# A two-layer decoder on one core: more of layer 0's output stage moved into its attention, and another order of the memory hops

## The reference

```
x = layernorm(x + quaternion_attention(x))      # 16 heads of 16, softmax over 1024 keys
x = layernorm(x + memory_hops(ctx, x, W0, W1))  # two hops over 77 context rows
x = layernorm(x + experts(x))                   # 8 experts, 256 rows each, gelu
x = layernorm(x + long_convolution(x))          # layer 1 starts here
x = layernorm(x + cross_attention(x, ctx))      # 16 heads
x = layernorm(x + quantised_gated_ffn(x))
```

## Time and profile before

| | |
|---|---|
| median of three runs | 780.7 us |
| the profiled execution | 774.46 us, span 772.7 us |
| PE matmul busy | 698.3 us, 90% |
| ACT busy | 557.5 us, 72% |
| DVE busy | 492.1 us, 64% |
| POOL busy | 193.3 us, 25% |
| mean granted TensorE clock | 0.986 |

### The profile page before, as it was taken

How to read it: one execution, slowest core, us unless ns; L and a number is a source line. 1 busy time by engine, 2 the same in 40 slices (tenths; PEclk the granted TensorE clock), 3 DMA queues, 4 the chain that set the end, 5 groups by cost and what they waited for, 6 DMA issues and landing times.

```text
span 772.7 us, 10924 instructions
## 1 busy us (share of the span) xinstructions
PE 698.3 (90%) x3854; PEld 383.6 (50%) x3854; DVE 492.1 (64%) x1156; ACT 557.5 (72%) x1071; POOL 193.3 (25%) x234
## 2 busy tenths in 40 slices
PE   4999999989999999989999999967988999993897
PEld 2652222212222223879888887633454644441686
DVE  4794645663422133669527666767887787988786
ACT  3759999999999997464242434799987633799991
POOL 1661143210110000203352232455554200000022
PEclk9999999999999999999999999999999999997899
DMA  7412112241157142203156000002000000000002
GB/s 195 140 31 49 30 28 69 28 96 28 28 111 230 29 115 77 102 8 111 46 172 215 5 0 1 1 1 82 7 35 1 1 1 0 1 0 0 1 27 82
DMA packets 58606, 42.27 MB, mean 55 GB/s; under 512 B 38226, under 2 KB 55352, under 8 KB 58424
## 3 DMA queue, kind: packets, MB, share of 16 engines
q1 hardware_dynamic: 58408, 41.44, 19.5%
q10 hardware_dynamic: 144, 0.13, 0.1%
HBM read 28.72 MB, written 4.46 MB: 43 GB/s over the span
## 4 chain that ended last, share of the span: by engine, by line
PE 55%; ACT 24%; DVE 15%; issue 3%; DMA 1%; SPq 1%; POOL 0%; POOLq 0%; ACTq 0%; DVEq 0%
ACT arena L665 12%; PE banks L1673 9%; PE banks L2210 8%; PE banks L1972 7%; PE banks L1988 6%; PE banks L1659 4%; ACT arena L790 4%; PE banks L1643 3%; DVE arena L1498 2%; DVE arena L1063 2%; PE banks L1833 2%; PE banks L1646 2%; DVE arena L1071 2%; PE banks L2002 1%; PE banks L1716 1%
## 5 line engine op out<-in xcount | busy, mean ns | idle before, releaser
L665 ACT ACTIVATE arena<-banks 128x1024 f32<-128x1024 f32 x256 | 239.8, 1047 | 6.7 <-PE banks L1673 4.2
L1673 PE MATMUL banks<-arena 128*32 128x512 f32 x1024 | 136.4, 604 | 2.6 <-DVE arena L1139 2.4
L1659 PE MATMUL banks<-arena 64*128 64x512 f16 x512 | 86.4, 383 | 10.3 <-ACT arena L665 5.8
L2210 PE MATMUL banks<-arena 128*128 128x512 f32 x192 | 83.1, 594 | 1.1 <-DVE arena L1514 0.9
L790 ACT ACTIVATE arena<-banks,arena 128x77 f32<-128x77 f32 x256 | 70.6, 403 | 13.9 <-DVE arena L1413 13.7
L414 POOL TENSOR_SCALAR arena<-arena 128x2 f32<-128x2 f32 (+2 forms) x39 | 11.8, 302 | 254.9 <-DVE arena L1066 254.9
L1659 PEld LDWEIGHTS banks<-arena 64*128 64x128 f16 x512 | 21.0, 93 | 108.8 <-ACT arena L665 98.9
L746 ACT ACTIVATE arena<-banks,arena 128x256 f32<-128x256 f32 x64 | 26.9, 471 | 49.3 <-PE banks L1972 49.3
L2210 PEld LDWEIGHTS banks<-arena 128*128 128x128 f32 x192 | 36.2, 190 | 47.4 <-issue 43.4
L1988 PE MATMUL banks<-arena 128*128 128x256 f32 x256 | 56.5, 380 | 1.2 <-ACT arena L687 1.2
L1972 PE MATMUL banks<-arena 128*128 128x256 f32 x256 | 56.2, 379 | 0.0
(11 more groups left out here) (255 smaller groups left out, 1253.4 us busy)
## 6 DMA issues: line engine op xcount, KB each, us to landing
arena<-in_L_ffn_w SPq DMA_DIRECT2D x16, 1024.0 KB, 7.5
w_kept<-arena SPq DMA_DIRECT2D x3, 768.0 KB, 3.6
arena<-w_kept SPq DMA_DIRECT2D x3, 768.0 KB, 4.4
arena<-in_x SPq DMA_DIRECT2D x4, 512.0 KB, 7.1
out_x<-arena SPq DMA_DIRECT2D x3, 512.0 KB, 2.9
arena<-in_L_ffn_b SPq DMA_DIRECT2D x1, 1024.0 KB, 14.9
arena<-in_L_ffn_w_gate SPq DMA_DIRECT2D x1, 768.0 KB, 7.6
arena<-in_L_ffn_w_up SPq DMA_DIRECT2D x1, 768.0 KB, 9.4
```

Of the source, the lines that this page charges most:

```text
L665: act.activation(PT[kt % 2][:, half], PS[:, 2 * (n % 3):2 * (n % 3) + 2, :], ACT.Exp, scale=DH ** -0.5 / QK_UP ** 2).then_inc(sem("exp_don ...
L1659: mm = pe.matmul(bank(2 * (n % 3) + h), KT[u % 2][64 * h:64 * h + 64, P * kt:P * kt + P], QT[u % 2][64 * h:64 * h + 64, 512 * half:512 * h ...
L1673: mm = pe.matmul(PS[32 * j:32 * j + 32, 6, :], VS[w][:, kt, h, :], PT[kt % 2][:, half, h, :], start=(kt == 0), stop=(kt == TB - 1))
L2210: mm = pe.matmul(bank(2 + n % 4), (wgT if n < IC * G4 else wuT)[:, k, P * c:P * c + P], XT[:, k, 512 * g:512 * g + 512], start=(k == 0), s ...
```

## The change

- Batch 0's output stage takes ten key steps for each q (Q_STEPS): turns at 0 and 2, the turn back at 4, projections at 5 to 8. It ends in unit 12. The turn of the next q waits for the residual's addition (first_y) instead of its statistics. VectorE's pieces, the quantisation of the last weight among them, are placed anew in units 8 to 13.
- Unit 13 turns groups 0 and 1 of the normalised rows (early_x_turn, steps 2, 4, 6, 7), copied by VectorE (early_x) instead of by ACT behind the attention.
- Unit 14 turns the first four of batch 1's head pairs, for all four q (early_turn, part 0), unit 15 the next three (part 1, steps 0, 2, 4, 6), and in it, at steps 3 and 5, two matrices of layer 1 (l1_turn 0 and 1, copied by VectorE in early_weight). They wait for the four matrix loads alone (l1_raw_in). All use bank 7. Behind the attention only the last head pair is turned (last_turn, last_heads).
- Behind the attention, scores of set 0 stand ahead of batch 1's output stage, and those of sets 1 and 2 right behind it. VectorE weaves minimum and weights into that stage. The hops have another order, and mem_residual(1), mem_stats(1) and mem_residual(2) stand ahead of the last mem_summed; before, they stood behind it. The first FFN matmul waits for two residuals instead of one.
- WpT, WqT and bc1 lie elsewhere in SBUF, and mem_output uses other banks.

The diff, cut to its core (indentation shortened; left out are SBUF places, the removed VectorE loop, ACT's list, and the removed functions of PE):

```diff
-MEM_ORDER = ((0, 0), (0, 1), (0, 2), (0, 3), (1, 0), (0, 4), (1, 1), (0, 5), (1, 2), (1, 3), (1, 4), (1, 5))
+MEM_ORDER = ((0, 0), (0, 1), (0, 2), (1, 0), (0, 3), (1, 1), (0, 4), (1, 2), (0, 5), (1, 3), (1, 4), (1, 5))
 MEM_AT = {item: i for i, item in enumerate(MEM_ORDER)}
-L1_BANK = (4, 5, 0, 0, 0)
-MEM_OUT = ((2, 2), (4, 3), (6, 5), (4, 6))
+L1_BANK = (7, 7, 0, 0, 0)
+MEM_OUT = ((2, 2), (2, 3), (4, 5), (6, 6))
 HT = 13
 SPREAD = {2: (0, 0), 4: (1, 0), 6: (0, 1), 8: (1, 1), 11: (0, 2), 13: (1, 2)}
+Q_STEPS = 10
+EARLY_X_AT = (2, 4, 6, 7)
+EARLY_AT = (0, 2, 4, 6)
+EARLY_L1_AT = (3, 5)
 UX = T * KD
...
+def early_x(g, k):
+    if k == 0:
+        dve.wait_ge(sem("x_tr"), T + g + 1)
+    else:
+        dve.wait_ge(sem("xg_tr"), MEM_X + g + 1)
+    dve.tensor_copy(XT[:, k, 512 * g:512 * g + 512], bank(7)).then_inc(sem("xgT" if k else "xT"), 1)
+def early_heads(part, i):
+    dve.wait_ge(sem("o_tr"), 9 + 4 * part + i)
+    n = 4 - part
+    o = bank(7)[:, 0:P * n].rearrange("p (u j w) -> p u j w", u=n, j=4)
+    link(dve.reciprocal(rden0[:, 0:n], o[:, :, :, DH]))
+    for half in range(2):
+        ins = dve.tensor_tensor(ATT1[:, i, half, P * part:P * part + 2 * DH * n].rearrange("p (u h d) -> p u h d", u=n, h=2),
+                                o[:, :, half::2, 0:DH], rden0[:, 0:n, half::2, None].to_broadcast([P, n, 2, DH]), ALU.mult)
+    ins.then_inc(sem("att"), 1)
...
+    dve.wait_ge(sem("o_tr"), 17)
...
+        ins = dve.tensor_tensor(ATT1[:, :, half, 2 * DH * (NP - 1):2 * DH * NP].rearrange("p q (h d) -> p q h d", h=2),
+                                o[:, :, half::2, 0:DH], rden0[:, :, half::2, None].to_broadcast([P, 4, 2, DH]), ALU.mult)
+    ins.then_inc(sem("att"), 1)
...
+def early_weight(n):
+    dve.wait_ge(sem("l1_wtr"), n + 1)
+    dve.tensor_copy((WpT, WqT)[n].rearrange("p k d -> p (k d)"), bank(7)).then_inc(sem("l1_wT"), 1)
...
+    if r < 4:
+        dve.sem_inc(sem("first_y"), 1)
...
         late_qn(HT if u == HT - TB else T - 1)
     if late < T and u % 2 == 1:
         late_v(late)
-    if u >= NP:
-        q = (u - NP) // 2
...
+    if u == NP:
+        first_heads(0, 0)
+        first_heads(0, 1)
+        quantised(2, 1)
+        first_turned(0)
+    if u == NP + 1:
+        out_residual(0, 7)
+        first_heads(1, 0)
+        out_norm(0)
+        quantised(2, 2)
+        first_heads(1, 1)
+        first_turned(1)
+    if u == NP + 2:
+        out_residual(1, 7)
+        first_heads(2, 0)
+        out_norm(1)
+        first_heads(2, 1)
+    if u == NP + 3:
+        first_turned(2)
+        out_residual(2, 7)
+        first_heads(3, 0)
+        out_norm(2)
+    if u == NP + 4:
+        first_heads(3, 1)
+        first_turned(3)
+        out_residual(3, 7)
+    if u == NP + 5:
+        out_norm(3)
+        for g in range(2):
+            for k in range(KD):
+                early_x(g, k)
+    if u == NP + 6:
+        for i in range(4):
+            early_heads(0, i)
+    if u == NP + 7:
+        early_heads(1, 0)
+        early_heads(1, 1)
+        early_weight(0)
+        early_heads(1, 2)
+        early_weight(1)
+        early_heads(1, 3)
     dve.wait_ge(sem("pv_done"), TB * u + TB)
     dve.tensor_copy(OSB[:, u], bank(6)).then_inc(sem("o_evac"), 1)
...
     view = lambda j: X[:, 4 * g + j, :]
     normalise(view, view, 4, 4 * (g % 2)).then_inc(sem("ln_b"), 1)
+last_heads()
 mem_lowest(0, 0)
+out_residual(4, 6)
+mem_weights(0, 0)
+out_residual(5, 7)
+out_norm(4)
+out_residual(6, 6)
+out_norm(5)
+out_residual(7, 7)
 mem_lowest(0, 1)
-mem_weights(0, 0)
+out_norm(6)
 mem_lowest(0, 2)
 mem_weights(0, 1)
+out_norm(7)
+mem_lowest(1, 0)
+mem_weights(0, 2)
 mem_lowest(0, 3)
-mem_weights(0, 2)
-mem_lowest(1, 0)
+mem_weights(1, 0)
+mem_lowest(1, 1)
 mem_weights(0, 3)
 mem_lowest(0, 4)
-mem_weights(1, 0)
-mem_lowest(1, 1)
+mem_weights(1, 1)
+mem_summed(0)
+mem_lowest(1, 2)
 mem_weights(0, 4)
 mem_lowest(0, 5)
-mem_weights(1, 1)
-mem_summed(0)
-mem_weights(0, 5)
-mem_lowest(1, 2)
+mem_weights(1, 2)
 mem_summed(1)
 mem_lowest(1, 3)
-mem_weights(1, 2)
-mem_weights(1, 3)
-mem_lowest(1, 4)
+mem_weights(0, 5)
 mem_residual(0)
 mem_summed(2)
 mem_stats(0)
+mem_lowest(1, 4)
+mem_weights(1, 3)
+mem_residual(1)
+mem_summed(3)
 mem_lowest(1, 5)
 mem_weights(1, 4)
-mem_summed(3)
+mem_norm(0)
+mem_stats(1)
+mem_summed(4)
 mem_weights(1, 5)
-mem_summed(4)
-mem_norm(0)
+mem_residual(2)
 mem_summed(5)
-mem_residual(1)
-mem_stats(1)
-mem_residual(2)
+mem_norm(1)
 mem_stats(2)
 mem_residual(3)
-mem_norm(1)
 mem_stats(3)
 mem_norm(2)
...
-        pe.wait_ge(sem("ln_stat"), LN_A + q)
+        pe.wait_ge(sem("first_y"), q)
...
-    if step == 9:
+    if step in (0, 2):
+        first_turn(q, step // 2)
+    if step == 4:
         first_att_turn(q)
-    if 11 <= step < 15:
-        first_proj(q, (step - 11) // 2, (step - 11) % 2)
+    if 5 <= step < 9:
+        first_proj(q, (step - 5) // 2, (step - 5) % 2)
+def early_x_turn(g, k):
...
+    if k:
+        pe.wait_ge(sem("xT"), T + g + 1)
+    elif g:
+        pe.wait_ge(sem("xgT"), MEM_X + g)
+    else:
+        pe.wait_ge(sem("ln_a"), 4)
+    for j in range(4):
+        mm = pe.transpose(bank(7)[:, P * j:P * j + P], X[:, 4 * g + j, P * k:P * k + P], ident)
+    mm.then_inc(sem("xg_tr" if k else "x_tr"), 1)
...
+def early_turn(part, i):
+    if part == 0:
+        if i == 0:
+            pe.wait_ge(sem("xgT"), MEM_X + 2)
+            pe.wait_ge(sem("o_evac"), NP + 4)
+        else:
+            pe.wait_ge(sem("att"), 8 + i)
+    elif i == 0:
+        pe.wait_ge(sem("att"), 12)
+        pe.wait_ge(sem("o_evac"), NP + 7)
+    elif i == 1:
+        pe.wait_ge(sem("att"), 13)
+    else:
+        pe.wait_ge(sem("l1_wT"), i - 1)
+    for n in range(4 - part):
+        mm = pe.transpose(bank(7)[:, P * n:P * n + P], OSB[:, NP + 4 * part + n, P * i:P * i + P], ident)
+    mm.then_inc(sem("o_tr"), 1)
+def l1_turn(n):
...
+    if n == 0:
+        pe.wait_ge(sem("l1_raw_in"), 16 * 4)
+    if n < 2:
+        pe.wait_ge(sem("att"), 14 + n)
...
+        if u == NP + 5 and kt in EARLY_X_AT:
+            i = EARLY_X_AT.index(kt)
+            early_x_turn(i // KD, i % KD)
+        if u == NP + 6 and kt in EARLY_AT:
+            early_turn(0, EARLY_AT.index(kt))
+        if u == NP + 7 and kt in EARLY_AT:
+            early_turn(1, EARLY_AT.index(kt))
+        if u == NP + 7 and kt in EARLY_L1_AT:
+            l1_turn(EARLY_L1_AT.index(kt))
...
+        mm = pe.transpose(bank(7)[:, P * i:P * i + P], OSB[:, UN - 1, P * i:P * i + P], ident)
+    mm.then_inc(sem("o_tr"), 1)
+def att_turn(q):
     if q == 4:
-        pe.wait_ge(sem("o_evac"), UN)
...
-x_group_turn("ln_a", 4, MEM_X, 0)
-l1_turn(0)
-l1_turn(1)
-x_group_turn("ln_a", 4, MEM_X + 1, 1)
+last_turn()
 mem_scores(0)
+att_turn(4)
+att_turn(5)
+out_proj(4)
+att_turn(6)
+out_proj(5)
+att_turn(7)
+out_proj(6)
+out_proj(7)
+mem_turn(0, 0)
 mem_scores(1)
-x_group_turn("ln_a", 8, MEM_X + 2, 2)
 mem_scores(2)
-x_group_turn("ln_a", 8, MEM_X + 3, 3)
+mem_hop(0)
+mem_turn(0, 1)
+x_group_turn("ln_a", 8, MEM_X + 2, 2, b0=6)
+mem_turn(0, 2)
+x_group_turn("ln_a", 8, MEM_X + 3, 3, b0=6)
+mem_hop(1)
 mem_scores(3)
-mem_turn(0, 0)
-mem_turn(0, 1)
-mem_hop(0)
+mem_turn(1, 0)
+mem_hop(2)
 mem_scores(4)
-mem_turn(0, 2)
-mem_hop(1)
 mem_turn(0, 3)
 mem_scores(5)
-mem_turn(1, 0)
-mem_hop(2)
+mem_turn(1, 1)
+mem_hop(3)
 mem_turn(0, 4)
-mem_hop(3)
-mem_turn(1, 1)
+mem_output(0)
+mem_turn(1, 2)
 mem_hop(4)
 mem_turn(0, 5)
-mem_output(0)
-mem_turn(1, 2)
+mem_output(1)
 l1_turn(2)
 mem_hop(5)
 mem_turn(1, 3)
 l1_turn(3)
-mem_output(1)
 mem_turn(1, 4)
+mem_output(2)
 l1_turn(4)
 mem_turn(1, 5)
-mem_output(2)
 def context_keys():
-    pe.wait_ge(sem("mem_y"), G4 - 1)
+    pe.wait_ge(sem("mem_y"), G4)
     for c in range(KD):
         for k in range(KD):
...
```

More of the change, by code:

```diff
@@ L223, in decoder @@
         nrm = [prj(2, DQ) for _ in range(2)]
-        a5 = at(16384, 20480)
-        ATT = [a5(2, D) for _ in range(2)]
+        ATT1 = at(18432, 20480)(4, 2, D)
+        a5 = at(16384, 17408)
         OT = [a5(2, KD, P) for _ in range(2)]
-        rden = [a5(NP, 4) for _ in range(2)]
         a6 = at(16384, 16384 + 8 * 256)
@@ L244, in decoder @@
         memS = zz(3, T)
-        WpT = zz(KD, D)
-        WqT = zz(KD, D)
         Kbd = zz(KD, B, HC, LC)
@@ L249, in decoder @@
         zz(B * KD * 3 * P)
-        bc1 = zz(4, D)
         hmask = zz(HC)
@@ L253, in decoder @@
         kTx = zz(B * LC)
+        z3 = at(28672 + 2 * 512 * 6 + 4 * 768)
+        bc1 = z3(4, D)
+        WpT = z3(KD, D)
+        WqT = z3(KD, D)
         cb = at(28672, 28672 + 4 * LC * G4 + B * KD * HC * LC)
@@ L678, in _, with turned_out @@
                 act.activation(ctxR[:, b, :, 2 * LC:REPEATED], rows[:, :, 0:REPEATED - 2 * LC], ACT.Copy).then_inc(sem("ctx_rep"), 1)
-            for q in range(4, 8):
+            def turned_out(q):
                 act.wait_ge(sem("at_tr"), q + 1)
@@ L682, in _ @@
                     act.wait_ge(sem("wo_mm"), q - 1)
```

(41 more changed lines are left out.)

84 lines of the change are left out of this document (26 added, 58 removed).

## The result

The changed kernel takes 788.45 us (median; 785.61 to 790.07), the kernel before, on the same chip, 780.83 us (780.52 to 781.76). The ratio is 1.0121, 95% interval 1.0083 to 1.0158. That is slower, as forecast, but by nearly twice the forecast 0.65%, and 780.7 x 1.0121 = 790.1 lies just above the range's upper end (781 to 790). The interval, 787.2 to 793.0 us, holds both sides of that end.

A forecast was written before the change was run, and what follows sets the result against it. Attention was taken as paced by ACT or, with inserts, PE; the stage behind by PE, then VectorE's list, then PE. Attention +2.5 and that stage +2.6 gave +5.1 on 780.7, so 785.8 us, range 781 to 790.

The forecast's parts named there:

- (a): Attention, units 8 to 12: batch 0's outputs at ten steps per row group take 80.3 us against 77.2, +3.0.
- (b): Attention, units 13 to 15: with 14 new inserts they take 46.6 us against 47.1, -0.5.
- The upper bound given for (a) and (b) together: Attention: every new insert at full price, nothing given back, 14 x 0.6 and the 3.0, less 1.0, stated as +9.
- (c): Stage behind the attention: FFN starts 51.4 us behind the last copy instead of 48.8, as VectorE's list grows, +2.6.
- The clock rival: Stage behind the attention: clock falls around PE's wait ahead of mem_output(2), about +4, total 790 us; chance 0.14.
- (d): Everything else, including SP, POOL, SBUF places and work behind the FFN's start: nothing moves, 0.

The follow-up runs named there:

- e7: Kernel before with only batch 0's output stage at ten key steps each, nothing new in units 13 to 15, stage behind as before; 778.52 us, ratio 0.9992.
- e4: Changed kernel with unit 13's four row turns at steps 1, 3, 5, 6 instead of 2, 4, 6, 7; 791.3 us, ratio 1.015; when repeated 788.48 us, 1.0124.
- e6: Changed kernel with six unused 128x256 matmuls on PE in the hole ahead of mem_output(2); 782.12 us, ratio 1.0047 to the kernel before.
- e3: Changed kernel with residual 1, statistics 1, residual 2 behind the last sum, sum 4 ahead of norm 0, mem_output(2) behind the last turn; 778.76 us, ratio 1.0000.
- e1: The kernel before, unchanged, run again as a control; 778.76 us, ratio 0.9991; profiled execution 778.8 us.

## Why the prediction came out as it did

- **(a) Ten steps, +3.0 predicted, +3.9 measured.** Right in kind, sized 0.8 low: 81.1 instead of 80.3 us for units 8 to 12. One source is in its own rows: a pair of steps with and without an insert is 264.84 - 261.13 = 3.71 us, not 3.65. By e7 the spacing costs 0.3 net, because units 13 to 15 give back 3.5 when they lose the last of batch 0's work.
- **(b) Units 13 to 15, -0.5 predicted, -0.5 measured**, and unit by unit: 16.27, 15.29, 15.04 against 16.3, 15.3, 15.0. The two VectorE copies back to back behind unit 13's last step are there (278.57, 279.18), and by e4 they cost the 1.1 us. The upper bound given for (a) and (b) together is added wrongly: 14 x 0.6 and 3.0, less 1.0, is 10.4 and not 9; nothing hangs on it.
- **(c) The stage behind, +2.6 predicted, +5.8 measured. This is the step that failed.** Its walk was good: norm 7 of the first layer ends at 18.1 (18.5), mem_output(0) ends at 33.8 (34.7), mem_output(2) waits 2.9 (3). At full clock (e6) the last sum ends at 47.4 (48.5) and the FFN starts at 50.1 (51.4). So without the clock it is +1.4 instead of +2.6, and 0.9 of that difference had come about by the first output. VectorE's list between that output and the last sum is 13.5 us against 13.7. The failure is that every duration behind the hole (output 2, the turn, output 3, the FFN's first matmuls) was taken at 2.4 GHz, with the fall of the clock put at nothing in the sum. The walk itself produced the 3 us hole on PE, in a stretch with little matmul work, and the clock fell in it: 4.4 us up to the FFN's start and 1.4 in its first group.
- **The clock rival** had the right place, mechanism and roughly the price (+4 up to the FFN), but a chance of 0.14, because the row with a fall that it read had no PE work at all and turns stood between these waits. In the traces with the hole those turns did not help: four of four fell. And there were other rows. The trace of the kernel before has two more waits of this kind, 2.21 and 3.00 us long between pieces of matmul work, and within 2 us behind each the clock went to 0.50 and stayed there for 3.4 us, in which PE was never idle (PE's timeline and windows of the kernel before):

```profile
534.89 1.06 PE L2036 MATMUL banks<-arena 128*128 128x128 f32 x8 [2.21 <-ACT arena L809]
...
536.50:539.50 3.00, 3.00 (x13) 1.44 (x9) 2.40 (x4) 3.00 (x15) 1.40 (x2) 0.50 0.00 0
...
589.77 0.79 PE L2058 MATMUL banks<-arena 64*128 64x308 f32 x4 [3.00 <-ACT arena L790]
...
591.00:594.00 3.00, 3.00 (x10) 2.64 (x11) 1.46 (x3) 3.00 (x15) 1.41 (x2) 0.50 0.00 0
```

They speak for a higher chance than 0.14 of a fall behind a hole of 3 us. That it would last two to four times as long here, they don't show.

The Trainium skill (Perfetto Trace Analysis, Matmul Optimizations) says that the engine scales its power with use and wants matmuls in back-to-back batches; the trace agrees (1.00 to 0.50), and e6 shows it from the other side.

- **(d)** The stages beyond the FFN's first group run as before: from the first to the last of the expert matmuls' starts it is 116.9 us, 115.5 where the clock is full at the start, the 1.4 named above.

The sum from common origins: 3.3 in the attention, 1.4 in the stage at full clock, 4.4 and 1.4 from the clock, 10.5 us. The timed ratios of 1.0121 and 1.0128 are 9.4 to 10 us of 780. About half of the loss is the clock's, shown by e6; the rest is the order of the tail (e3 wins it back) and the inserts in units 13 to 15 (e7 is without them). The forecast of +5.1 is close to the +4.7 that is left without the clock (e6's timed 1.0047 is 3.7 us), but in part by luck: the attention was taken 0.8 too low and the stage 1.2 too high. What stays open is why the half-clock stretches behind 500 us vary.

## What to carry to other kernels

When your own walk through the queues puts a hole on PE between pieces of sparse matmul work, reckon everything behind it twice, at full and at half clock, and give the second a chance to match. Look in the trace that you have for waits of that length and for the clock behind them. Then see first whether another order closes the hole, because six unused matmuls in it won 6 us here, and moving three VectorE pieces and one output won 10. Work that an engine does under somebody else's long stage is free only there: three pieces ahead of a sum that PE waits for cost 4.1 us. And a stage's gain of about 1 us can be read in a trace long before it shows in a total whose executions differ by several.

## What was not expected of the hardware

- A hole of 2.91 us on PE, with 0.38 us of matmuls in the 2 us around its start, took the clock from 2.4 to 1.2 GHz; it stayed there for 10 to 14 us in three of the four profiled executions with the hole (6.8 in the fourth), while PE was busy for most of it. The price was 2.5 to 5.9 us, up to twice the hole itself. Two waits of the kernel before, 2.21 and 3.00 us, had a fall behind them too, of 3.4 us each.
- In one execution the stretches at half clock come to 21.5 us (before, 774.5 us), in another of the same kernel to 38.3 (e1, 778.8 us), with stages of equal length outside them.
- A matmul written as one 128x256 f32 product is two instructions in the trace (12 became x24, 5.34 us, 0.22 each), which doubled the price of the filler.
